# A state-space input stage: one of eight convolution taps on GpSimd instead of VectorE

## What is computed

```python
h = x @ fc1_w.T + fc1_b
xz = h @ in_proj_w.T
xc, z = jnp.split(xz, 2, axis=-1)                 # 256 channels each
xp = jnp.pad(xc, ((0, 0), (d_conv - 1, 0), (0, 0)))
u = sum((xp[:, w:w + L, :] * conv_w[:, w] for w in range(d_conv))) + conv_b   # d_conv = 4
u = jax.nn.silu(u)
x_dbl = u @ x_proj_w.T
dt_low, Bm, Cm = jnp.split(x_dbl, [dt_rank, dt_rank + d_state], axis=-1)
dt = jax.nn.softplus(dt_low @ dt_proj_w.T + dt_proj_b)
# then the scan over time with dt, A, Bm, Cm and u, gated with silu(z)
```

## Time and profile before

| | us |
|---|---|
| median of 3 runs | 1456.65 |
| lowest, highest | 1452.21, 1457.52 |
| the profiled execution: time | 1461.46 |
| the profiled execution: span in the profile | 1459.3 |

### The profile page before, as it was taken

The page is one execution under the profiler, slowest core; times in us unless marked ns, Lnnn a source line. Parts: engine busy times, 40 slices in busy tenths (PEclk is TensorE's granted clock), DMA queues, the critical chain, the costliest instruction groups (busy, mean ns, idle before and its releaser), DMA issues. The chain is left out here.

```text
span 1459.3 us, 21367 instructions
## 1 busy us (share of the span) xinstructions
PE 1215.0 (83%) x7478; PEld 548.7 (38%) x7478; DVE 1151.0 (79%) x1366; ACT 672.7 (46%) x1057; POOL 652.0 (45%) x468
## 2 busy tenths in 40 slices
PE   4937899999899899899968767877877877866998
PEld 2412343343334354445433212322322322355565
DVE  4869899999897458675557789999999999964554
ACT  2514899899798532132226863323333333302221
POOL 2320001000112166567651269989989979920000
PEclk9956999999999899999978959989989989985999
DMA  4321112312112263234510023423433333200331
GB/s 106 120 97 38 51 52 63 102 52 77 51 39 69 51 156 112 88 111 112 114 33 0 11 90 130 130 89 128 130 118 113 119 125 118 99 28 10 65 58 44
DMA packets 75346, 120.37 MB, mean 82 GB/s; under 512 B 13246, under 2 KB 42758, under 8 KB 75254
## 3 DMA queue, kind: packets, MB, share of 16 engines
q1 hardware_dynamic: 73958, 117.83, 27.4%
q10 hardware_dynamic: 1296, 1.33, 0.3%
HBM read 105.09 MB, written 13.63 MB: 81 GB/s over the span
## 5 line engine op out<-in xcount | busy, mean ns | idle before, releaser
L638 DVE TENSOR_REDUCE att_found<-PS 128x2 f32<-128x1024 f32 (+2 forms) x288 | 333.3, 1218 | 19.5 <-PE PS L747 17.7
L1796 PE MATMUL PS<-ms_ch,ident_sb 128*128 128x512 f32 x512 | 277.0, 668 | 71.2 <-POOL ms_ch L1903 71.2
L714 ACT ACTIVATE att_prob<-PS 128x512 f32<-128x512 f32 x576 | 313.6, 596 | 46.9 <-PE PS L769 34.9
L1903 POOL TENSOR_TENSOR ms_ch<-xnT,ms_c_rows 128x1024 f32<-128x1024 f32 x128 | 303.0, 2378 | 46.3 <-PE PS L1796 25.5
L1861 DVE TENSOR_TENSOR_SCAN xnT<-ms_decay,PS 128x1024 f32<-128x1024 f32 x96 | 216.1, 2275 | 4.2
L788 PE MATMUL PS<-att_prob,att_v 128*32 128x256 f32 (+1 forms) x2560 | 185.7, 377 | 2.8 <-ACT fr_out L703 2.6
L1796 PEld LDWEIGHTS PS<-ms_ch,ident_sb 128*128 128x128 f32 x512 | 100.6, 208 | 196.2 <-POOL ms_ch L1903 106.2
L1834 ACT ACTIVATE PS<-m_dt,m_a 128x1024 f32<-128x1024 f32 x32 | 35.8, 1118 | 263.4 <-DVE xnT L1861 263.4
L747 PE MATMUL PS<-kr,qr 55*128 55x128 bf16 (+4 forms) x1152 | 121.9, 293 | 30.9 <-PEq L260 15.6
L769 PE MATMUL PS<-qr,kr 55*128 55x128 bf16 (+4 forms) x1152 | 115.9, 279 | 15.1 <-ACT att_prob L714 8.2
L1848 DVE TENSOR_TENSOR PS<-ms_dtu,PS 128x1024 f32<-128x1024 f32 x96 | 115.1, 1214 | 9.6 <-PE PS L1787 9.3
(11 more groups left out here) (222 smaller groups left out, 1679.1 us busy)
## 6 DMA issues: line engine op xcount, KB each, us to landing
ms_c_rows<-bc_rows_dram SPq DMA_DIRECT2D x64, 512.0 KB, 5.9
f_gate_row<-gate_rows_dram SPq DMA_DIRECT2D x64, 256.0 KB, 3.5
ms_b_row<-bc_rows_dram SPq DMA_DIRECT2D x32, 512.0 KB, 3.6
f_mask_row<-mask_rows_dram SPq DMA_DIRECT2D x64, 128.0 KB, 3.1
qk_parts_dram<-qkv_parts SPq DMA_DIRECT2D x48, 128.0 KB, 1.9
heads_dram<-fr_out SPq DMA_DIRECT2D x16, 256.0 KB, 2.7
f_mask_row<-mask_rows_dram SPq DMA_DIRECT2D x64, 64.0 KB, 3.3
qr<-qk_parts_dram SPq DMA_DIRECT2D x32, 96.0 KB
```

What stands on the lines that cost most here:

```text
L638: dve.tensor_reduce(found[:, :, pair, first:first + (n - 1) * step + 1:step], PS[:, bank:bank + 2, :].rearrange("p r (w n) -> p r w n", w= ...
L714: act.activation(prob[:, step % PROB_RING * GH + h, :], PS[:, SCORE_BANK + unit % SCORE_RING, :], ACT.Exp, scale=float(D) ** -0.5).then_in ...
L1796: last = pe.matmul(PS[:, Y_BANK + 2 * half + q, :], g.ident[:, :], ch[:, half, q * CH:(q + 1) * CH], start=j == 0 and not odd, stop=j == J ...
L1903: pool.tensor_tensor(ch[:, half, :], h[:, odd, half, :], c_rows[:, s % C_RING, :], ALU.mult).then_inc(ch_ready, 1)
```

## The change

GpSimd gets a loop of its own ahead of its second part: per chunk it waits for the same two conditions as VectorE and multiplies the first tap of the second half, with the column of weights broadcast along the free dimension, into conv. A new semaphore, half_taps, counts these products. VectorE leaves this product out, so it has seven steps per chunk (CONV is 7), and its first fused tap of the second half waits for half_taps. The first fused tap of the first half has only one marked step before it and waits for that.

```diff
+        half_taps = sem("half_taps")
...
-        CONV = KC * DI
+        CONV = KC * DI - 1
...
                 for k in range(CPB):
                     c = CPB * b + k
 
+                    pool.wait_ge(xc_ready, 1 + 3 * b + 1 + 2 * k)
+                    pool.wait_ge(u_ready, DI * (c + 1))
+                    pool.tensor_tensor(conv[:, k, 1, :], xc[:, k, 1, 0:CH], conv_w[:, 1, 0:1].to_broadcast([P, CH]), ALU.mult).then_inc(half_taps, 1)
+            with pool.Fori(0, B) as b:
+                for k in range(CPB):
+                    c = CPB * b + k
+
                     pool.wait_ge(part2_ready, c + 1)
...
                     for tap in range(KC):
                         for half in range(DI):
                             x, w = xc[:, k, half, tap:tap + CH], conv_w[:, half, tap:tap + 1]
-                            if tap == 0:
+                            if tap == 0 and half == 0:
                                 steps.mark(dve.tensor_scalar(conv[:, k, half, :], x, w, None, ALU.mult))
-                            else:
-                                dve.wait_ge(conv_steps, steps.base + steps.n - 1)
+                            elif tap > 0:
+                                if half == 0:
+                                    dve.wait_ge(conv_steps, steps.base + max(steps.n - 1, 1))
+                                elif tap == 1:
+                                    dve.wait_ge(half_taps, c + 1)
+                                else:
+                                    dve.wait_ge(conv_steps, steps.base + steps.n - 1)
                                 steps.mark(dve.scalar_tensor_tensor(conv[:, k, half, :], x, w, conv[:, k, half, :], ALU.mult, ALU.add))
```

## The result

The changed kernel takes 1460.62 us (median of 19 runs) against 1456.28 us for the kernel before (19 runs): ratio 1.0030, 95% interval 1.0019 to 1.0041, or 4.3 us more. The forecast was + 6.0 us and 1462.6 us. The profiled execution took 1465.02 us with a span of 1462.8.

The account below looks back on a forecast made before the run. VectorE, busy 38.22 of 38.25 us in the convolution, was taken as the bound. Per chunk -0.40 + 0.115 + 1.03 = +0.745 us, times 8 = +6.0 us on 1456.65, gave 1462.6 us; range 1456.5 to 1467.5.

Parts of the forecast that it names:

- part 4: Convolution: VectorE's fused taps and GpSimd's product take turns reading SBUF, costing VectorE 1.03 us per chunk (0.88 to 1.09).
- What bounds: VectorE bounds the convolution; its gain or loss there reaches the kernel's end one for one unless ScalarE becomes the bound.
- a loss outside 774 to 820 us: Sign in the changed profile: time lost outside the convolution's stretch would make the whole argument wrong.
- Part 1: Convolution: one of VectorE's two first taps per chunk goes, 0.40 us less per chunk, 3.2 us in all.
- Part 2: Convolution: first fused tap of half 0 now waits for its immediate predecessor, losing 0.115 us per chunk, 0.9 in all.
- Part 3: Convolution: GpSimd's product is ready in time, no semaphore cost from chunk 1 on; perhaps 0.1 us once in chunk 0.
- The slope of 2.13 ns per element: Pricing VectorE's hold from GpSimd's product lengths, (2354 - 1265) / 512: 1.09 us for 512 elements.
- four times the loss of 128 elements: Pricing VectorE's hold by scaling: 0.49 us for two GpSimd products of 128 elements, four times the mean, 0.98 us.
- the first (no turns): Rival: fused taps run undisturbed beside GpSimd's product; -2.3 us, 1454.4 us (-0.16%); chance 0.12.
- The second (GpSimd starved): Rival: product runs only when VectorE stands still at half_taps, 1.38 us per chunk; +8.8 us, 1465.4 us; chance 0.12.
- the tight wait: Convolution: the first fused tap of half 0 waiting for the step just before it; 0.115 us per chunk.
- The third (the whole recorded length: Rival: GpSimd's product holds VectorE for its full 1.265 us per chunk; +7.8 us, 1464.5 us; chance 0.11.

Follow-up runs that it names:

- the second profile of the same changed kernel: The changed kernel run again without any edit, beside the kernel before: 1460.34 us, ratio 1.0027.
- ScalarE's version: Changed kernel with the halves of later taps swapped and the product on ScalarE instead of GpSimd: 1454.16 us, ratio 0.9983; repeated, 1455.73 us, ratio 0.9992.
- done alone: Kernel before with only one edit: the first fused tap of half 0 waits for the step just before it; one run, 1458.38 us.
- the sister kernels: Kernel before plus a GpSimd product into an unread tile (1463.91 us), the same with 256 elements (1460.30), changed kernel with later taps' halves swapped (1461.19).
- a full tile: Changed kernel with the weights spread beforehand into a real 128x512 tile as GpSimd's second input, instead of a broadcast column; one run, 1464.03 us.
- the unread product: Kernel before, VectorE still doing all eight taps, plus a GpSimd product into a tile nobody reads: 1463.91 us, ratio 1.0049.
- the half: Kernel before, all eight taps on VectorE, plus a GpSimd product of 256 instead of 512 elements into a tile nobody reads; one run, 1460.30 us.
- The tensor_scalar: Changed kernel with GpSimd's product as a tensor_scalar, one input stream and a column of scalars, instead of a tensor_tensor: 1458.99 us, ratio 1.0018.
- a memset: Kernel before, all eight taps on VectorE, plus a GpSimd memset of 512 elements per chunk into a tile nobody reads; one run, 1453.27 us.

## Why the prediction was right, and which term was off

The mechanism was the forecast one, and the time lies in the range, on the side of "within 0.5%". By the steps:

- **The time.** The measured 1460.62 us lie 0.8 under the lowest of the forecast's own sums (1461.4), because part 4 was priced too high. The range reached down to 1456.5, 4.9 us under that sum and not the 2 us of scatter named for it, so a loss near nothing would have lain in it as well, and that the time lies in it says little by itself.
- **What bounds.** VectorE's convolution passed its change on to the end: 4.15 us in the stage, 4.3 us in the time. In the profile the second part then ran 1.3 us longer (from the last tap to the scan's first product 45.88 us, before 44.61) and the scan gave 1.4 us back, from its first product of that line to its last. I had named a loss outside 774 to 820 us as a sign against the argument. This one is not the change's: the second profile of the same changed kernel has 43.68 us there, 2.2 less, and again a stage of 42.39 us. The granted clock of TensorE was 0.88 in the stage and 0.80 behind it, where 0.92 and 0.77 stood before.
- **Part 1,** 0.40 us per chunk: 4.37 us per chunk on ScalarE's version. Right.
- **Part 2,** 0.115 us: 0.125 when done alone. Right.
- **Part 3,** the product is in time: VectorE never waits at half_taps. Right, also in chunk 0, where product and first tap began together; the product held the first tap by 0.86 us, its price and no more. The small real wait that I had allowed in chunk 0 did not come, and the product took 1.04 us where I had 1.265. It depends on GpSimd getting its turn, which it did not everywhere in the sister kernels.
- **Part 4,** the turn: right in kind, off in size. This is the term that was mis-sized: "I take 1.03" was 0.79 in seven chunks and 0.86 in the first. Two steps failed. The slope of 2.13 ns per element came from products of two full tiles; this one reads a broadcast column, with a slope of 1.7, and for a full tile the loss was 0.84 or 1.01 us by buffer. And four times the loss of 128 elements (0.98) does not carry over: per element the loss was 1.9 ns at line 1894 (0.245 / 128), but 1.3 for 256 elements (0.34 / 256) and 1.5 for 512 (0.79 / 512) beside the taps. Line 1894 has the form of the new product but not its size, and the VectorE instruction beside it was another; which of these makes it dearer no run shows.

With measured terms the sum closes: 8 x (-0.40 + 0.115) + 7 x 0.79 + 0.86 = + 4.1 us.

Of the rivals, the first (no turns) is refuted by the held taps of 1531 ns and by the unread product, which costs 7 us. The second (GpSimd starved) did not happen in the changed kernel but did for a third of the products without the tight wait, at 1.0 to 1.1 us for each of 512 elements instead of my 1.38. The third (the whole recorded length, which I had taken as 1.265 us) fails on the changed kernel itself, 0.79 lost for an undisturbed 1.04 us, and on the half, 0.34 lost for 0.61. The tensor_scalar agrees, but its length by itself is not known.

## What to carry to other kernels

An idle GpSimd is no free helper for a VectorE that is busy all the time. Here a GpSimd product of 1.04 us took 0.79 us from a VectorE that read two SBUF tensors, and 0.86 from a tap that read only one. So moving a tap of 0.40 us there cost 0.79 us, while the same tap on ScalarE held no tap of VectorE's. Before moving work to GpSimd, look for a place in the trace where both engines read SBUF, take the loss from a GpSimd instruction of the same size and form as the new one, and check whether ScalarE has the room.

## What the runs showed that I had not expected

- GpSimd's tensor_scalar of 128x512 with a column of scalars was recorded at 1.71 us at the least, its tensor_tensor with the same column broadcast at 1.04 us. The instruction with one stream is the longer record and holds VectorE for less, 0.36 to 0.6 us instead of 0.79. How long it takes with VectorE idle no run shows.
- A GpSimd product may be passed over by a VectorE that is never idle: 4.53 us from start to end for 1.04 us of work. Eight of 24 products without a tight wait on VectorE, none of 32 with one.
- A first tap, which reads one SBUF tensor, is held by GpSimd too: for 0.86 us by the product in the changed kernel, and for 0.32 us (0.79 instead of 0.47) by a memset, which reads nothing and held no fused tap. SBUF — State Buffer of the Trainium skill, section "Who interferes with whom", says that VectorE's two-port modes contend with any GpSimd instruction and a VectorE instruction with two SBUF inputs only with one that reads SBUF. The 48 fused taps beside the memsets agree with the second; the first would account for the held first tap if that tap runs in such a mode, which no run here shows.
